# A two-layer transformer kernel: the second layer's attention scores in three passes of split operands

## The reference, cut to what matters

```
k, q, v = x@Wk.T, x@Wq.T, x@Wv.T        # x: layer-normed residual of 512 tokens
ak = k @ Wa.T
alpha = softmax(q @ ak.T)               # the scores: 512 x 512 for each of 8 chunks
x = x + alpha @ (v @ Wb.T)
```

## Time and profile before

| | us |
|---|---|
| median of 3 runs | 972.42 (970.34 to 974.18) |
| profiled execution, its own time | 970.89 |
| its span, first to last instruction | 969.1 |
| PE busy | 919.5 (95%) |
| DVE, POOL, ACT busy | 685.0, 592.3, 555.7 |
| score matmuls (L761), 64 records | 33.2 |

### The profile page before, as it was taken

The page is one execution under the profiler, slowest core; times in us unless marked ns, Lnnn a source line. Parts: engine busy times, 40 slices in busy tenths (PEclk is TensorE's granted clock), DMA queues, the critical chain, the costliest instruction groups (busy, mean ns, idle before and its releaser), DMA issues. The chain is left out here.

```text
span 969.1 us, 17609 instructions
## 1 busy us (share of the span) xinstructions
PE 919.5 (95%) x5060; PEld 698.9 (72%) x5067; DVE 685.0 (71%) x2098; ACT 555.7 (57%) x1255; POOL 592.3 (61%) x565
## 2 busy tenths in 40 slices
PE   6999999999999999999999999889998999989996
PEld 3777777777777767777767776568994676658996
DVE  5657678888888797888898787474542567665553
ACT  4444655766757577674664443135663676635663
POOL 5678868868577586776867876544441244552443
PEclk8899999999999999999999999999999999999999
DMA  6890000000000000000000000435544000005552
GB/s 182 356 404 2 1 1 1 1 1 1 1 1 1 1 1 1 2 0 1 12 1 12 13 1 27 146 105 179 180 148 119 2 13 23 24 32 152 179 178 87
DMA packets 39774, 62.74 MB, mean 65 GB/s; under 512 B 7073, under 2 KB 23266, under 8 KB 37504
## 3 DMA queue, kind: packets, MB, share of 16 engines
q1 hardware_dynamic: 35136, 53.08, 16.7%
q0 software_dynamic: 4544, 8.54, 2.6%
HBM read 34.68 MB, written 27.82 MB: 64 GB/s over the span
## 5 line engine op out<-in xcount | busy, mean ns | idle before, releaser
L384 PE MATMUL bank<-split 128*128 128x512 f32 x544 | 244.0, 448 | 5.8 <-POOL split L1816 3.0
L386 PE MATMUL bank<-split 128*128 128x512 f32 x544 | 214.9, 395 | 0.0
L385 PE MATMUL bank<-split 128*128 128x512 f32 x544 | 213.8, 393 | 0.0
L909 ACT ACTIVATE sil<-bank 128x512 f32<-128x512 f32 x128 | 76.0, 594 | 147.2 <-PE bank L386 146.7
L384 PEld LDWEIGHTS bank<-split 128*128 128x128 f32 x544 | 103.0, 189 | 36.0 <-issue 10.4
L385 PEld LDWEIGHTS bank<-split 128*128 128x128 f32 x544 | 103.4, 190 | 26.3 <-issue 10.5
L1295 DVE TENSOR_TENSOR act<-bank,sil 128x512 f32<-128x512 f32 x128 | 87.7, 685 | 48.3 <-PE bank L386 25.4
L386 PEld LDWEIGHTS bank<-split 128*128 128x128 f32 x544 | 102.9, 189 | 23.8
L1772 POOL TENSOR_TENSOR act<-act 128x512 f32<-128x512 f32 x64 | 88.6, 1384 | 27.9 <-DVE act L1301 27.7
L1778 POOL TENSOR_TENSOR split<-act,split 128x512 fp32r<-128x512 f32 x64 | 89.7, 1403 | 16.5 <-ACT split L976 16.2
L735 PE MATMUL bank<-xlT,e 128*128 128x128 f32 x624 | 84.2, 278 | 7.8 <-ACT hT_e L1172 4.5
(11 more groups left out here) (314 smaller groups left out, 2010.7 us busy)
## 6 DMA issues: line engine op xcount, KB each, us to landing
e<-e_dram SPq DMA_DIRECT2D x78, 256.0 KB
rows_in<-yw SPq DMA_DIRECT2D x17, 1056.0 KB, 17.9
xin<-rows_in SPq DMA_DIRECT2D x78, 66.0 KB
e<-e_dram SPq DMA_DIRECT2D x4, 512.0 KB, 7.9
x<-rows_out SPq DMA_DIRECT2D x8, 256.0 KB, 4.6
rows_in<-yw,slot_i POOLq DMA_INDIRECT x64, 2.3
rows_out<-ob,ids POOLq DMA_INDIRECT x39
out<-ob,ids POOLq DMA_INDIRECT x39
```

The costliest lines, as they stand in the source:

```text
L384: mm(dst, w[0], m[0], start=start, stop=False, **more)
L385: mm(dst, w[0], m[1], start=False, stop=False, **more)
L386: return mm(dst, w[1], m[0], start=False, stop=stop, **more)
L909: af(sil[(k - 1) % 2][:, :], bank[BH1[STEPS[k - 1][0] % 2]][:, :], ACT.Silu).then_inc(silu_done.sem, 1)
```

## The change

Only the second layer's scores go over to `mm3`, with z as the stationary operand and y as the moving one. The parts are kept in a new tile `yz` (two buffers of high and low for y and for z). The high parts are copies rounded by ACT in `y_G`: z's from bank 7 in place of the float32 copy of L1207, y's as a second copy behind it. The low part of z is formed by DVE from bank 7 (`z_rest`, between share_of(2) and `y_stats`), that of y by POOL (after the scaling of chunk n, before the scatters). The score waits for both; `y_U`, which overwrites bank 7, waits for z's low part instead of the copy. Three pairs of semaphores are merged, among them two around the bias table between first layer and expert tiles. The merge puts DVE's wait for the products ahead of `bias_parts` instead of behind it.

```diff
 # PE, score(n)
                     pe.wait_ge(*exp_done(main, n - 1))
-                    mm(bank[n % 2][:, :], zT[p][:, rows(n)], yT[p][:, :], start=True, stop=True).then_inc(sc_ready.sem, 1)
+                    pe.wait_ge(*y_low(main))
+                    pe.wait_ge(*z_low(main))
+                    mm3(bank[n % 2][:, :], tuple(z_[:, rows(n)] for z_ in zsT[p]), ysT[p], True, True).then_inc(sc_ready.sem, 1)
 # PE, y_G and y_U
-                    pe.wait_ge(*yT_saved(pre))
+                    pe.wait_ge(*yT_saved(pre, 1))
-                    pe.wait_ge(*zT_saved(pre))
+                    pe.wait_ge(*z_low(pre))
 # ACT, y_G
                     act.wait_ge(*zT_ready(pre))
-                    af(zT[pre % 2][:, :], bank[7][:, :], ACT.Copy).then_inc(zT_saved.sem, 1)
+                    act.wait_ge(*sc_ready(pre - 2))
+                    af(zsT[pre % 2][0], bank[7][:, :], ACT.Copy).then_inc(zT_saved.sem, 1)
+                    af(ysT[pre % 2][0], yT[pre % 2][:, :], ACT.Copy).then_inc(yT_saved.sem, 1)
 # DVE
+                def z_rest():
+                    if pre is None:
+                        return
+                    dve.wait_ge(*zT_saved(pre))
+                    v.tensor_tensor(zsT[pre % 2][1], bank[7][:, :], zsT[pre % 2][0].bitcast(F32), ALU.subtract).then_inc(z_low.sem, 1)
                 share_of(2)
+                z_rest()
                 y_stats()
 # DVE, between first layer and expert tiles
             tables(0)
+            dve.wait_ge(late_made.sem, 4)
             bias_parts()
-            dve.wait_ge(prod_saved.sem, 4)
 # POOL, second_layer_slot, after the scaling of st and before r_scatter(srt)
+                if pre is not None:
+                    pool.wait_ge(*yT_saved(pre))
+                    pool.tensor_tensor(out=ysT[pre % 2][1], in0=yT[pre % 2][:, :], in1=ysT[pre % 2][0].bitcast(F32), op=ALU.subtract
+                                       ).then_inc(y_low.sem, 1)
                 r_scatter(srt)
```

More of the change, by code:

```diff
@@ L159, in build @@
         yn_l = [yn_f, yn_a]
-        zT, pr_, pT = mT1, act0[0:2], act0[2:4]
+        pr_, pT = act0[0:2], act0[2:4]
         vu = [z, h2]
@@ L187, in build @@
         waT = sb("waT", [P, P]); wbT = sb("wbT", [P, P])
+        yz = sb("yz", [P, 8 * S], F32R)
+        ysT, zsT = ([tuple(yz[:, (4 * i + 2 * k + b) * S:(4 * i + 2 * k + b + 1) * S] for b in range(2)) for i in range(2)] for k in range(2))
         wak = sb("wak", [P, P]); gmat = sb("gmat", [P, P]); wuT = sb("wuT", [P, P])
@@ L222, in build @@
         routing_constants, rows_zeroed = sem("routing_constants", 8 + E), sem("rows_zeroed")
-        prod_ready, prod_saved, scaled, hT_low, weight_high, weight_low, weight_rest = (
-            sem("prod_ready"), sem("prod_saved"), sem("scaled"), sem("hT_low"), sem("weight_high"), sem("weight_low"), sem("weight_rest"))
-        bn_f, stat_f, rstd_f, normed_f, ynT_f = sem("bn_f", 4), sem("stat_f"), sem("rstd_f", 2), sem("normed_f"), sem("ynT_f")
+        prod_ready, late_made, scaled, hT_low, weight_high, weight_low, weight_rest = (
+            sem("prod_ready"), sem("late_made"), sem("scaled"), sem("hT_low"), sem("weight_high"), sem("weight_low"), sem("weight_rest"))
+        bn_x, stat_f, rstd_f, normed_f, ynT_f = sem("bn_x", 4), sem("stat_f"), sem("rstd_f", 2), sem("normed_f"), sem("ynT_f")
         t_ready, t_low, logits_ready, top2_steps = sem("t_ready"), sem("t_low"), sem("logits_ready"), sem("top2_steps", 9)
@@ L257, in build @@
         wts_in = [sem(f"wts_in{i}", 16) for i in range(WT)]
-        e2_loaded, eb2_steps = sem("e2_loaded"), sem("eb2_steps", 6)
+        e2_loaded = sem("e2_loaded")
         tile_T, xlT_saved, hid_ready, relu_act, relu_dve, o_ready, ob_ready = (
@@ L264, in build @@
         fetched = [sem(f"fetched{i}", 16) for i in range(NCH)]
-        bn_l, stat_l, rstd_l, normed_l, ynT_l = (
-            sem("bn_l", 4), sem("stat_l"), sem("rstd_l", 2), sem("normed_l"), sem("ynT_l"))
+        stat_l, rstd_l, normed_l, ynT_l = sem("stat_l"), sem("rstd_l", 2), sem("normed_l"), sem("ynT_l")
         yT_saved, zT_ready, zT_saved, v1_ready, v1_saved = (
-            sem("yT_saved"), sem("zT_ready"), sem("zT_saved"), sem("v1_ready"), sem("v1_saved"))
+            sem("yT_saved", 2), sem("zT_ready"), sem("zT_saved"), sem("v1_ready"), sem("v1_saved"))
         sc_ready, nmax_done, exp_done, pT_ready, pT_saved = (
             sem(n, 4) for n in ("sc_ready", "nmax_done", "exp_done", "pT_ready", "pT_saved"))
+        y_low, z_low = sem("y_low"), sem("z_low")
         rsum_done, ao_ready, ao_done = sem("rsum_done", 4), sem("ao_ready", 4), sem("ao_done", 4)
@@ L401, in products @@
                 tr(bank[3][:, 0:E * J], eb1r[:, :], ident[0:E * J, 0:E * J]).then_inc(prod_ready.sem, 1)
-                pe.wait_ge(prod_saved.sem, 1)
+                pe.wait_ge(late_made.sem, 1)
                 mm(bank[2][:, 0:P], wq_l1[:, :], wak[:, :], start=True, stop=True).then_inc(prod_ready.sem, 1)
-                pe.wait_ge(prod_saved.sem, 4)
+                pe.wait_ge(late_made.sem, 4)
             def first_layer(s):
@@ L865, in _ @@
             keep_busy(9)
-            pe.wait_ge(*eb2_steps(0))
+            pe.wait_ge(late_made.sem, 10)
             pe.wait_ge(e2_loaded.sem, 16 * len(e2_loads))
@@ L893, in products @@
                 act.wait_ge(prod_ready.sem, 2)
-                af(wak[:, :], bank[0][:, 0:P], ACT.Copy).then_inc(prod_saved.sem, 1)
-                af(wuT[:, :], bank[1][:, 0:P], ACT.Copy).then_inc(prod_saved.sem, 1)
+                af(wak[:, :], bank[0][:, 0:P], ACT.Copy).then_inc(late_made.sem, 1)
+                af(wuT[:, :], bank[1][:, 0:P], ACT.Copy).then_inc(late_made.sem, 1)
                 act.wait_ge(prod_ready.sem, 3)
-                af(eb1T[:, :, :].rearrange("p e j -> p (e j)"), bank[3][:, 0:E * J], ACT.Copy).then_inc(prod_saved.sem, 1)
+                af(eb1T[:, :, :].rearrange("p e j -> p (e j)"), bank[3][:, 0:E * J], ACT.Copy).then_inc(late_made.sem, 1)
                 act.wait_ge(prod_ready.sem, 4)
-                af(gmat[:, :], bank[2][:, 0:P], ACT.Copy).then_inc(prod_saved.sem, 1)
+                af(gmat[:, :], bank[2][:, 0:P], ACT.Copy).then_inc(late_made.sem, 1)
             def first_layer(s):
@@ L1245, in _ @@
             products()
-            act.wait_ge(prod_saved.sem, 4)
+            act.wait_ge(late_made.sem, 4)
             tiles(0, 2, expert)
@@ L1318, in f_stats @@
                         dve.wait_ge(*xa_done(n - NCH))
-                    moments(xc(n), stats_f, bn_f)
+                    moments(xc(n), stats_f, bn_x)
                     dve.wait_ge(*normed_f(n - 2))
-                    aggregate(n, stats_f, part_f, mv_f[n % 2], -0.5, bn_f, stat_f, [(sc_f[n % 2][:, 0, :], *RMS)])
+                    aggregate(n, stats_f, part_f, mv_f[n % 2], -0.5, bn_x, stat_f, [(sc_f[n % 2][:, 0, :], *RMS)])
                 def top2(i):
@@ L1632, in chain @@
                 def chain(ins, n):
-                    ins.then_inc(eb2_steps.sem, 1)
-                    dve.wait_ge(*eb2_steps(0, n))
+                    ins.then_inc(late_made.sem, 1)
+                    dve.wait_ge(late_made.sem, 4 + n)
                 dve.wait_ge(late_loaded.sem, 16 * len(late_loads))
@@ L1647, in bias_parts @@
                 chain(v.tensor_tensor(eb2r[96:96 + E, :], eb2r[96:96 + E, :], eb2p[96:96 + E, :], ALU.subtract), 5)
-                v.tensor_copy(eb2p[96:96 + E, :], eb2r[96:96 + E, :]).then_inc(eb2_steps.sem, 1)
+                v.tensor_copy(eb2p[96:96 + E, :], eb2r[96:96 + E, :]).then_inc(late_made.sem, 1)
             def expert(n0, n1, n2):
@@ L1697, in y_stats @@
                     dve.wait_ge(*fetched[st](0))
-                    moments(xc(st), stats_l, bn_l)
+                    moments(xc(st), stats_l, bn_x)
                     dve.wait_ge(*normed_l(st - 2))
-                    aggregate(st, stats_l, part_l, mv_l[st % 2], -0.5, bn_l, stat_l, [(sc_l[st % 2][:, 0, :], *PLAIN)])
+                    aggregate(MAINS + st, stats_l, part_l, mv_l[st % 2], -0.5, bn_x, stat_l, [(sc_l[st % 2][:, 0, :], *PLAIN)])
                 maximum(0)
```

## The result

| | before | after |
|---|---|---|
| median of 6 runs, side by side | 971.87 (970.34 to 974.18) | 979.31 (977.17 to 980.65) |
| profiled execution, its own time | 970.89 | 980.25 |
| its span | 969.1 | 978.5 |
| PE, DVE, POOL, ACT busy | 919.5, 685.0, 592.3, 555.7 | 917.9, 690.3, 602.7, 560.2 |

The changed kernel is slower: ratio 1.0078, 95% interval 1.0062 to 1.0094, so +7.4 us of medians. PE has less to do, 1.6 us of 919.5, and the kernel takes longer.

The account below looks back on a forecast made before the run. Score(0), then DVE's queue, then PE were taken to set a slot. Beginning +3.48, five slots +3.15, two slots gaining 0.34 each: +5.95; with clock 1.0, 972.42 + 6.95 = 979.4 us, range 974.7 to 985.0.

Parts of the forecast that it names:

- The chain of a slot: Score(0) through score(3), `z_rest`, statistics and POOL's subtraction to the next score(0): 14.77 us instead of 14.15.
- PE's idle time at the slot's head: Before score(0), PE waits 0.96 us for POOL's subtraction.
- The scores: Each score 0.17 us cheaper, only two of four in a slot on the path: -0.34 us a slot.
- rival 2: All 32 scores lie on PE's path and nothing new is waited for: -5.4 us, 967.0; chance 0.04.
- ACT's second copy: y's rounded copy in ACT's queue takes 0.60 us, covered by 0.89 us idle before the last exponential.
- `z_rest`: On DVE ahead of the statistics, 0.61 us start to start, bounds 0 and 0.69.
- the subtraction: On POOL behind the wait for the statistics, 1.27 us, other bound 2.21; the next score(0) waits for it.
- rival 3: DVE and POOL hold each other up, the subtraction takes 2.21 us in six slots: +5.6, 985.0; chance 0.12.
- The beginning: In slot 1 the statistics of chunk 1 stand behind `z_rest`: score(0) of chunk 0 +4.34 us, chunk 1's +3.48.
- The clock: PE idles in slot 1, so a fall to half clock is likely there: +1.0 us, bounds 0 and 1.87.
- the slots: Five more slots, main 1 to 5, end with the subtraction: 5 x 0.63 = 3.15 us.
- the last two slots: In main 6 and 7 POOL reaches the subtraction early, and each slot gains 0.34 us.

Follow-up runs that it names:

- experiment 1: The changed kernel with POOL's subtraction for y moved ahead of its wait for the next chunk's statistics; median 972.45, ratio 1.0020 to the kernel before.
- experiment 4: The changed kernel with POOL's subtraction for y done twice in a row, the second releasing PE; 987.13, ratio 1.0179 to the kernel before.
- experiment 5: The changed kernel with `z_rest` behind `y_stats` on DVE in all slots; 972.87, ratio 1.0014 to the kernel before.
- experiment 6: Experiment 2's kernel with all four scores as one float32 product of z's rounded copy, the splitting kept; 972.62, ratio 1.0011 to the kernel before.
- experiment 7: Experiment 2's kernel with only score(1) and score(2) as one float32 product of z's rounded copy; 970.24, ratio 0.9988 to the kernel before.
- experiment 3: The changed kernel with 14 matmuls on constants, results unused, behind y_U in the slot without attention; 978.53, ratio 1.0090 to the kernel before.
- experiment 8: Experiment 2's kernel with unused matmuls on constants before y_U in the slot without attention and before y_T in chunk 0's; 970.22, ratio 0.9987 to the kernel before.
- experiment 2: Experiment 1's kernel with the statistics ahead of `z_rest` in the slot without attention; 969.98, ratio 0.9998 to the kernel before.
- experiment 10: The kernel before, float32 scores, with DVE's maximum(1) and share_of(0) moved ahead of the routing's statistics and factors; 965.01, ratio 0.9944 to the kernel before.

## Why the prediction was right

*The chain of a slot.* From the maximum of score(3) on, every step stands in the timeline at its place, counted from score(0): that maximum 8.84 (forecast 8.77), `z_rest` 9.52 (9.44), statistics 10.11 (10.05), L1948 12.14 (12.07), L1951 13.23 (13.16), subtraction 13.38 (13.42), its end 14.65 (14.69), next score(0) 14.75 (14.77). The step ahead of them came out by two errors that cancel: score(3) shows at 7.55, not 7.87 (its first record begins while y_G's second one still runs, and lasts 0.79 us where the other scores' last 0.47), and its maximum 1.29 behind it, not 0.90. Over the five slots from chunk 1 to chunk 6 the loss grew by 2.97; the forecast had 3.15. Experiments 1, 4 and 5 moved, doubled and shortened this chain, and the slot followed each time by the sum of its rows, to 0.03 us.

*PE's idle time at the slot's head* is shown as 0.69 to 0.91, not 0.96. Part of the rest stands before weight_T(1), where PE waited 0.73 in place of 0.57. Taken away (experiment 1) the wait gave back 0.98.

*The scores.* That only two of the four lie on the path was argued from one idle place before; experiments 6 and 7 show it, with 0.31 a slot for the two. So rival 2, all 32 scores on the path, fell.

*The copies and subtractions.* ACT's second copy 0.62 (0.60), `z_rest` 0.59 from start to start in the slot shown (0.61), the subtraction, by its line's durations (min/median/max ns):

```profile
L1954 POOL TENSOR_TENSOR yz<-tT,yz x4: 1262/1268/1269, 748.3 to 835.8; 128x512 fp32r<-128x512 f32 x4
...
L1954 POOL TENSOR_TENSOR yz<-hT,yz x4: 1264/1271/1280, 762.5 to 846.5; 128x512 fp32r<-128x512 f32 x4
```

1262 to 1280 ns in all eight: the 2213 ns of the earlier trace rows did not come back, and rival 3 fell. By the Trainium skill ("SBUF — State Buffer", Who interferes with whom) DVE and GpSimd hold each other up where a DVE instruction takes two inputs from SBUF; in the slot shown DVE's work beside the subtraction is its adds at 806.02 and 806.98, which take one of their inputs from a bank, and the trace agrees with the page as far as it goes. No row shown has a DVE instruction of the page's kind beside it.

*The beginning.* +4.23 for +4.34, by the same steps: `z_rest` 744.42, the statistics 745.02, L1948 747.06, subtraction 748.29, score(0) 749.66.

*The clock is the one term mis-sized.* From score(0) of chunk 0 to that of chunk 1 the loss grew by 0.53 (4.76 - 4.23), where the beginning's own working had it shrink by 0.86. The difference, 1.39, is the fall's price in this place, for which I took 1.0 (bounds 0 and 1.87); experiment 3's distance, 1.32 shorter with no fall there, gives nearly the same, and its two slots with a fall are 1.55 and 1.58 longer than after's. The forecast's reading of the earlier trace rows was not whole: ahead of that fall PE also ran matmuls of 512 columns, on constants, from 620.23. What a fall costs over a whole execution stays open (experiments 3 and 8).

*The sum.* The stage lost 7.11 in the trace, the forecast had 6.95; the medians lost 7.44. The errors of the terms are -0.11 for the beginning, +0.39 for the clock, -0.18 for the slots and +0.06 for the last two slots: small, and partly against each other. That the median of 979.31 lies only 0.1 from the forecast time is luck: the loss was 0.49 larger than forecast, and the kernel before came out 0.55 below the 972.42 that the forecast added it to.

*Left open.* Why the median of experiment 1 is 1.9 above before, with a stage that is 0.5 shorter in its profile, is argued from the mean clock only. Experiment 2 is 2.5 below experiment 1, and its beginning accounts for 0.96 of that; the rest has no row. Its mean clock was higher, 0.990 against 0.988, but no run here sets the clock by itself.

## What to carry to other kernels

An engine that isn't busy is not an engine that is free: POOL was idle for half of each slot, and the work added to it came late because it stood behind a wait that had nothing to do with it. So place added work in each in-order queue by when its operands are there and who waits for it, ahead of unrelated waits; here that one place was worth 0.98 us a slot, and the order of two DVE lines 0.64. Before a product is made cheaper, look at what the engine does right behind it: in front of an idle place the gain is nothing, and the idle place itself (here DVE's order, worth 6 us in experiment 10) is the thing to change.

## What the runs showed of the hardware

The falls of the granted clock move. In the profiled executions of these kernels, stretches at 0.50 (1.2 GHz) of some 3 to 7 us begin in the second layer fifteen times, from 740 to 849 us; experiment 4's profile has four of them, those of before and of experiments 7 and 10 none. In the rows shown PE had stood idle just before (748 to 749 in after, 763 to 764 in experiment 3), and the half clock lasts on while PE is busy all the time (766 to 767). By the Trainium skill ("TensorE: Matmul & The Clock Gate", Part 1) idling halves the clock, and these rows agree. But the length of one idle time does not tell whether a fall follows: in experiment 4 PE was idle for 2.03 to 2.12 us ahead of score(0) of chunks 2 to 6, and falls began at 778, 826 and 843, behind chunks 2, 5 and 6, not behind 3 and 4 (809.83); ahead of experiment 8's fall at 846 its longest idle time in that slot was 0.69. Over 35 executions of the kernel before, the time rose by some 0.6 us for each 0.001 that the mean granted clock was lower (correlation -0.57), so about a third of the variance of these times, from 968 to 975 us, goes with the clock. To keep PE busy at one place (experiments 3 and 8) moved no median by more than the noise.
